# One launch of attention and experts: first two stages joined, four stored blocks a side, second key stack loaded by DMA

## Time and profile before

| | |
|---|---|
| median of 3 runs | 1906.98 us |
| the profiled execution | 1909.95 us |
| its span | 1908.0 us |
| TensorE busy | 87% of the span |
| VectorE, ScalarE, GpSimd busy | 73%, 60%, 56% |
| mean DMA rate | 237 GB/s |
| spread and project end, attend begins | 195.6 us |
| mix begins | 1396.6 us |
| experts begin | 1592.5 us |

### The profile page before, as it was taken

How to read it: one execution, slowest core, us unless ns; L and a number is a source line. 1 busy time by engine, 2 the same in 40 slices (tenths; PEclk the granted TensorE clock), 3 DMA queues, 4 the chain that set the end, 5 groups by cost and what they waited for, 6 DMA issues and landing times. The chain is left out here.

```text
span 1908.0 us, 41019 instructions
## 1 busy us (share of the span) xinstructions
PE 1656.5 (87%) x13688; PEld 1140.5 (60%) x13688; DVE 1390.5 (73%) x3938; ACT 1151.0 (60%) x2745; POOL 1071.8 (56%) x1268
## 2 busy tenths in 40 slices
PE   1883289999999999999999999999944755999997
PEld 1442056666666666666666666666523645999996
DVE  1573099999999999999999999999823652434343
ACT  1673258888888888887887888888622540222221
POOL 0210187787787787787787787787403521333332
PEclk9997589999999999999999999999976765999998
DMA  3599788878788878778888778878259823676772
GB/s 106 183 301 306 221 287 285 282 261 286 259 259 291 281 258 287 262 257 289 286 257 282 267 257 278 270 258 278 64 126 275 268 76 137 210 215 215 224 211 74
DMA packets 320830, 452.57 MB, mean 237 GB/s; under 512 B 38204, under 2 KB 260303, under 8 KB 320526
## 3 DMA queue, kind: packets, MB, share of 16 engines
q1 hardware_dynamic: 308034, 414.42, 67.6%
q10 hardware_dynamic: 7596, 21.10, 3.6%
q0 software_dynamic: 4992, 14.43, 2.1%
HBM read 256.87 MB, written 193.27 MB: 236 GB/s over the span
## 5 line engine op out<-in xcount | busy, mean ns | idle before, releaser
L872 ACT ACTIVATE t_probsT<-t_flip 128x512 f32<-128x512 f32 x1024 | 626.2, 614 | 200.3 <-PE t_flip L766 141.8
L817 DVE TENSOR_REDUCE t_most<-t_scores 128x1 f32<-128x640 f32 (+1 forms) x512 | 435.4, 850 | 58.1 <-PE t_scores L743 54.5
L836 DVE TENSOR_SCALAR t_band<-t_band,t_top 128x384 f32<-128x384 f32 (+1 forms) x512 | 415.5, 812 | 0.0
L780 PE MATMUL t_sum_ps<-t_probsT,t_vals 128*32 128x256 f32 x4096 | 327.2, 391 | 0.2 <-ACT t_probsT L872 0.2
L864 ACT COPY t_table<-t_table_ps 128x388 f32<-128x388 f32 x512 | 247.9, 484 | 65.3 <-issue 40.9
L949 POOL TENSOR_TENSOR t_near<-t_near,t_masks 128x768 f32<-128x768 f32 (+1 forms) x128 | 270.4, 2113 | 0.0
L821 DVE CUSTOM_DVE_ANT_0 t_band<-t_scores,t_near 128x384 f32<-128x384 f32 (+1 forms) x512 | 262.0, 512 | 0.0
L766 PE MATMUL t_flip<-t_masks,t_band 128*128 128x128 f32 x1408 | 260.6, 274 | 0.0
L736 PE MATMUL t_scores<-t_after,t_quest 105*128 105x256 bf16 (+3 forms) x1024 | 243.3, 287 | 3.8 <-DVE t_most L821 3.6
L743 PE MATMUL t_scores<-t_masks,t_near 128*128 128x128 f32 x1408 | 241.1, 274 | 1.6 <-POOLq L952 1.5
L743 PEld LDWEIGHTS t_scores<-t_masks,t_near 128*128 128x128 f32 x1408 | 180.7, 142 | 40.9 <-POOLq L952 2.8
(11 more groups left out here) (187 smaller groups left out, 2569.7 us busy)
## 6 DMA issues: line engine op xcount, KB each, us to landing
skew_d<-t_table SPq DMA_DIRECT2D x128, 1024.0 KB, 7.1
t_near<-skew_d SPq DMA_DIRECT2D x128, 640.0 KB, 8.1
t_near<-skew_d SPq DMA_DIRECT2D x128, 384.0 KB, 6.4
e_w<-in_L_ffn_W_dram ACTq DMA_DIRECT2D x39, 512.0 KB
e_w<-in_L_ffn_W_dram SPq DMA_DIRECT2D x39, 512.0 KB
split_d<-p_part SPq DMA_DIRECT2D x32, 384.0 KB
t_after<-split_d SPq DMA_DIRECT2D x64, 192.0 KB
t_quest<-split_d SPq DMA_DIRECT2D x64, 192.0 KB
```

Of the source, the lines that this page charges most:

```text
L780: last = nc.tensor.matmul(sum_ps[32 * g:32 * g + 32, 0:2 * P], vals[b % 2][:, j, h * VDIM:h * VDIM + 32], probsT[s % 3][:, g * 2 * P:(g + ...
L817: nc.vector.tensor_reduce(most[:, c, 1:2], out[:, wide:S], AX.X, ALU.max)
L836: nc.vector.tensor_scalar(band[n % 2][:, t, 0:wide], band[n % 2][:, t, 0:wide], top[n % 2][:, t:t + 1], None, ALU.subtract).then_inc(level ...
L872: nc.scalar.activation(probsT[s % 3][:, half * 512:(half + 1) * 512], flip_ps[half][:, :], ACT.Exp, scale=SCALE).then_inc(expd, 1)
```

## The change

1. spread goes, and its work is done at the beginning of project, in project's buffers. posT_d goes too, and the columns of far_w are written in SBUF. The masks are loaded once, kept in one buffer for all blocks, and so are the rows of pick_d. ScalarE's copy of the first turned group (L501) moves ahead of the next group's normalisation. The semaphores of project are cleared in attend behind the first loads.
2. xn_d, its loads in mix and GpSimd's addition go. 1 / deviation of each token stays in SBUF (inv_all), and mix adds x * inv_all instead of xn, with two instructions of VectorE for one. (The mean's share is the same for all features of a token, and falls out in the normalisation that follows.) bo is added by a matmul with a row of ones, two a group.
3. split_d has four blocks a side instead of six, so a group is stored with eight transfers instead of twelve, and the far parts with one instead of four.
4. A stack of 96 rows is loaded by two transfers of 48, each with three blocks on the DRAM side, and where a part is wanted three times the step of that dimension is 0. before is loaded in the same way; twin goes. The far rows of two units come together, in three transfers (load_far).

```diff
-QSLOTS = ((0, 1, 3), (3, 1, 2), (5, 1, 1))
-KSLOTS = ((1, 2, 3), (2, 2, 2), (0, 1, 1))
+BLOCKS = 4
+QSLOTS = ((0, 3, 4), (1, 5), (2,))
+KSLOTS = ((0, 1, 2), (3, 5), (4,))
...
-        spread(nc, sem, Wk, bk, rel_emb, c_pick, c_masks, c_side, pick_d, posT_d)
...
 # project, SyncE
-                    for m in range(4):
-                        for n, (first, step, many) in enumerate((QSLOTS, KSLOTS)[m // 2]):
-                            at = ((m // 2 * TERMS + first) * (N * DH) + b * D + m % 2 * P) * S + half * G
-                            sp.dma_start(view(split_d, at, [[S, P], [step * N * DH * S, many], [1, G]]),
-                                         part[g % 2][:, n, m, :].unsqueeze(1).to_broadcast([P, many, G])
-                                         ).then_inc(split_out[g % 2], 16)
+                    for m in range(4):
+                        mine = at + m // 2 * (BLOCKS * part_at) + m % 2 * (P * S)
+                        takes = ((0, 3, 1), (0, 1, 0)) if m < 2 else ((0, 3, 0), (1, 2, 3))
+                        for a, z, slot in takes:
+                            sp.dma_start(view(split_d, mine + slot * part_at, [[S, P], [part_at, z - a], [1, G]]),
+                                         part[g % 2][:, a:z, m, :]).then_inc(split_out[g % 2], 16)
...
 # project, ScalarE
+            def keep_x(g):
+                act.wait_ge(x_turned, g + 1)
+                if g >= 2:
+                    act.wait_ge(v_made, g - 1)
+                nc.scalar.copy(xT[g % 2][:, :, :], xT_ps[:, :, :]).then_inc(xT_made, 1)
...
             for s in range(-2, NG + 1):
+                if s == -1:
+                    keep_x(0)
...
 # attend
-    HATS = 5
+    HATS = 6
+    FARS = 2
+    ROW = DH * PARTS
...
-                for dst, side_at in ((after[i], TERMS * part), (quest[i], 0)):
-                    sp.dma_start(dst[0:KROWS, :], view(split_d, side_at + n * (DH * S), [[part, TERMS], [S, DH], [1, S]])
-                                 ).then_inc(hats_in[i], 16)
-                for dst, far_at, many in ((quest[i][FAR:FAR + 6, :], n * (2 * far), 2 * PARTS),
-                                          (after[i][KROWS:FAR, :], (N + n) * (2 * far) + far, PARTS),
-                                          (before[i][KROWS:FAR, :], (N + n) * (2 * far), PARTS)):
-                    sp.dma_start(dst, view(far_d, far_at, [[S, many], [1, S]])).then_inc(hats_in[i], 16)
+                at_q, at_k = n * (DH * S), BLOCKS * part + n * (DH * S)
+                for dst, at, step in ((after[i][0:ROW, :], at_k, 0), (after[i][ROW:KROWS, :], at_k + part, part),
+                                      (quest[i][0:ROW, :], at_q + part, part), (quest[i][ROW:KROWS, :], at_q, part),
+                                      (before[i][0:ROW, :], at_k, 0), (before[i][ROW:KROWS, :], at_k + part, part)):
+                    sp.dma_start(dst, view(split_d, at, [[step, PARTS], [S, DH], [1, S]])).then_inc(hats_in[i], 16)
+
+            def load_far(n):
+                i = n % BUFS
+                if n >= BUFS:
+                    sp.wait_ge(flipped, 2 * QT * (n + FARS - BUFS))
+                far_q = ((n // H * 4 + n % H // 8) * 32 + n % 8 * 2) * far
+                far_k = far_q + 2 * 32 * far
+                for dst, far_at, many in ((quests[FAR:FAR + 6, i:i + FARS, :], far_q, 2 * PARTS),
+                                          (afters[KROWS:FAR, i:i + FARS, :], far_k + far, PARTS),
+                                          (befores[KROWS:FAR, i:i + FARS, :], far_k, PARTS)):
+                    sp.dma_start(dst, view(far_d, far_at, [[S, many], [2 * far, FARS], [1, S]])
+                                 ).then_inc(far_in[i // FARS], 16)
...
                     load_unit(u + 4)
+                if 0 <= u + 2 < N and u % FARS == 0:
+                    load_far(u + 2)
...
-            def twin(n):
-                i = n % BUFS
-                act.wait_ge(hats_in[i], 16 * HATS * (n // BUFS + 1))
-                nc.scalar.copy(before[i][0:KROWS, :], after[i][0:KROWS, :]).then_inc(twin_made, 1)
...
 # mix, VectorE
-                nc.vector.tensor_tensor(y1[g % BUFS][:, :, :], out_ps[g % 2][:, :, :], xn[g % BUFS][:, :, :],
-                                        ALU.add).then_inc(y1_made, 1)
+                for t in range(G):
+                    tile = g * G + t
+                    last = nc.vector.scalar_tensor_tensor(y1[g % BUFS][:, t, :], xt[g % XBUFS][:, t, :],
+                                                          inv_all[:, tile:tile + 1], out_ps[g % 2][:, t, :], ALU.mult, ALU.add)
+                last.then_inc(y1_made, 1)
...
 # mix, TensorE
+                    last = nc.tensor.matmul(out_ps[g % 2][:, t, :], masks[0:1, 3, :], bo_row[:, :], start=False, stop=True)
...
 # experts, SyncE
-                if s == 0:
-                    sp.dma_start(masks[:, :, :], c_masks).then_inc(loaded, 16)
```

More of the change, by code:

```diff
@@ L115, in build @@
         bias_d, total_d = dram("bias_d", [E, HID]), dram("total_d", [E, D])
-        spread(nc, sem, Wk, bk, rel_emb, c_pick, c_masks, c_side, pick_d, posT_d)
[L118 to L122, removed]
+        masks = ctx.enter_context(nc.sbuf_tensor("masks", [P, 5, P], F32))
+        inv_all = ctx.enter_context(nc.sbuf_tensor("inv_all", [P, NT], F32))
+        with nc.sbuf_tensor("rows", [KROWS, H, 2, FEW], BF16) as rows:
+            project(nc, sem, x, Wq, bq, Wk, bk, Wv, bv, rel_emb, c_pick, c_masks, c_side, pick_d, split_d, far_d, v_d,
+                    masks, inv_all, rows)
+            spent = sem.spend()
+            attend(nc, sem, spent, masks, rows, split_d, far_d, v_d, skew_d, ctx_d)
         sem.take_back(spent)
@@ L273, in project @@
-def project(nc, sem, spent, x, Wq, bq, Wk, bk, Wv, bv, bo, c_masks, posT_d, xn_d, split_d, far_d, v_d):
+def project(nc, sem, x, Wq, bq, Wk, bk, Wv, bv, rel_emb, c_pick, c_masks, c_side, pick_d, split_d, far_d, v_d,
+            masks, inv_all, rows):
     G = 512
@@ L333, in load @@
                              ).then_inc(x_in[g % XB], 16)
[L335 to L340 removed]
+            front = [(rel[:, :], rel_emb), (masks[:, :, :], c_masks), (wk[:, :, :], Wk.rearrange("(k p) n -> p k n", p=P)),
+                     (bk_row[:, :], bk.rearrange("(a n) -> a n", a=1)), (side[:, :, :], c_side),
+                     (pick[:, 0, :], c_pick[0, :, :]), (pick[:, 1, :], c_pick[1, :, :])]
+            assert len(front) == 7
+            loads = [(wq[:, :, :], Wq.rearrange("(k p) n -> p k n", p=P)),
                      (wv[:, :, :], Wv.rearrange("(k p) n -> p k n", p=P)),
@@ L547, in _, with attend @@
                 last.then_inc(far_made, 1)
-        @block.gpsimd
-        def _(pool):
-            pool.wait_ge(loaded, 16 * 9)
-            for g in range(NG):
-                pool.wait_ge(xn_made, GT * (g + 1))
-                if g >= 2:
-                    pool.wait_ge(xn_out[g % 2], 16 * (g // 2))
-                nc.gpsimd.tensor_tensor(xnb[g % 2][:, :, :], xn[g % NB][:, :, :],
-                                        bo_b[:, :].unsqueeze(1).to_broadcast([P, GT, D]), ALU.add).then_inc(xnb_made, 1)
-def attend(nc, sem, spent, c_masks, split_d, far_d, v_d, pick_d, skew_d, ctx_d):
+def attend(nc, sem, spent, masks, rows, split_d, far_d, v_d, skew_d, ctx_d):
     AHEAD = 2 * QT + QT // 2
```

293 lines of the change are left out of this document (121 added, 172 removed).

## The result

The changed kernel takes 2043.9 us in the median of four runs (2041.7 to 2046.0), the kernel before 1906.8: a ratio of 1.0715, 95% interval 1.0697 to 1.0734. It is slower by 137 us; the forecast was 2039. The profiled execution took 2043.8 us, its span is 2042.0, against 1909.95 and 1908.0.

A forecast was written before the change was run, and what follows sets the result against it. TensorE sets the pace, DMA is runner-up; after the change three DMA engines would bind attention. 1909.95 - 59 + 198 + 3 - 8 - 2 = 2042 us profiled, 2039 as median; range of 8 in 10: 1940 to 2190.

The forecast's parts named there:

- The front: Before attend: first product at 20 us instead of 53.2, groups at 12.4 us, attend beginning 59 us earlier.
- Attention: Loads on three DMA engines slow each unit from 17.8 to 21.0 us: +198 us over 62 units, bounds 105 and 347.
- +3 for the start: First skew transfers of attention stand behind a load of 8 us instead of 2.7: +3 us (0 to 6).
- my two ends: Time of one of the three engines per attention unit: 19.5 us from below, 23.4 us from above.
- near 0.2 for some 8 us a unit: Sign in attention that the forecast is right: DMA share stays near 3 of 16 for some 8 us each unit.
- mix: Fewer xn transfers outweigh the added bo matmuls: -8 us, from -14 to +5.
- +2: In mix, the two added bo matmuls a group cost 2 us, counted only in the last four groups.
- experts: Masks no longer stand before the first total in SyncE's queue: -2 us, from -4 to 0.
- (a): Attention loads do not bind, by a wrong three-engine spread or air in the queue: 1838 us, chance 0.09.
- (b): In attention ScalarE holds TensorE back, hidden by busy time, and loads do not bind: 1771 us, chance 0.01.
- (c): In attention waits for near let TensorE's clock fall, units taking 25 us: 2297 us, chance 0.12.
- (d): Three engines bind in attention, but the front gains only its start: 2060 us, chance 0.78 together with the forecast.

The follow-up runs named there:

- 318 kB with 16 engines: The changed kernel with the rows of a stack reordered, so each load has outer dimension 16 instead of 3: 1869.8 us (ratio 0.9796).
- the kernel with 16 and twin: The changed kernel with loads of outer dimension 16, and before copied by ScalarE again instead of loaded: 1860.8 us (ratio 0.9750).
- bo first: The changed kernel with loads of outer dimension 16, ScalarE's copy of before restored, and mix's bo matmuls ahead of the wait for heads: 1839.8 us (ratio 0.9640).
- the attention part alone: The kernel before with six loads of 48 rows a unit, outer dimension 3, no step 0, and twin removed: 2090.3 us (ratio 1.0946).

## Why the prediction was right, point by point

**The front: right.** First product at 19.61 (20), groups of 12.4 us (34.43 to 46.82), last parts stored from 127.23 (127.6), attend's first load at 135.60 (137), and -60.0 for -59. The last stores were a little quicker than 0.81 us an issue: 4.43 us for eight. That ScalarE's chain holds at the start of attend held too: it copies first at 154.41, 5.6 us behind TensorE's first table.

**Attention: right in mechanism, a little large.** +198 and +3 for the start stood against +185.5: 20.8 us a unit for 21.0, and nothing seen of the 3. The engines ran at 23.0 GB/s (478 kB in 20.8 us), between my two ends of 24.5 (478 kB in 19.5) and 20.4. My 21.0 lay between the two ends by choice, and that it came so close is partly luck. I had put the distance from the low end down to idle engines, but with 4 of 1040 rows under 0.19 little of it seems to be that; more likely an engine carries less in the mixed traffic of a unit than in the rows that I had taken, which no run shows apart. The sign "near 0.2 for some 8 us a unit" was too long: 226 of the 1040 rows are at 0.26 or below, 4.5 us a unit, since the skew transfers overlap the loads. What stays open is why 318 kB with 16 engines cost 11 us and 347 kB in the kernel before none: its mean share is 0.89 for 0.82 and GpSimd waits 108 us for near instead of 9, so a second limit, that of the whole queue, may lie close. I left it out when I wrote that to drop twin is worth nothing: to replace it by loads costs 9 us, even with 16 engines.

The Trainium skill, "DMA: Bandwidth & Descriptors", section "Why a DMA increments its semaphore by 16 and not by 1", has the number of engines as the largest up to 16 that divides the slowest dimension of both sides. The trace agrees with it for 6 (0.39), 3 (0.19 to 0.21) and 2 (0.12, 0.13).

**mix: wrong in sign, -8 forecast and +16.2 measured.** The step that failed is "+2" for the bo matmuls. I saw them as free in all but the last four groups, because TensorE waited 3 to 4 us of each group for transfers, and put +5 as upper end with them on the path of all. Sixteen groups of 2.44 us are 39, so that end was far too low for what it named. Measured: mix +16.2, and 26 us less without the matmuls (on the kernel with 16 and twin, whose mix is 1 us longer). Two things took the cover away. VectorE's residual waits for the group's last matmul, and it stands ahead of the next heads, so bo behind the products lengthens a chain through two engines even while TensorE has idle time. And TensorE stayed at 0.50 up to 1655 us, where the kernel before reached 0.91. With bo first the chain gets shorter and the clock higher at once, so no run tells how much is due to each. Rows of the kernel before, PE, PEld, DVE, ACT, POOL busy, clock, share, GB/s:

```profile
1461.00:1495.00 34.00, 20.50 (x72) 16.35 (x72) 16.60 (x73) 16.18 (x36) 14.87 (x12) 0.65 0.92 290
1509.00:1528.00 19.00, 16.39 (x130) 12.46 (x130) 14.02 (x54) 12.92 (x29) 11.17 (x9) 0.91 0.85 281
```

The rest of the term came out about right: with no bo matmul mix takes 102.7 us, 9 less than in the kernel before, for the 10 (7 and 3) that I had put for the transfers that go; no run takes these transfers alone. My 8.8 us a group was that of groups 7 to 10 only: from the product of group 4 (1446.18) to that of 11 (1503.37) it was 8.2. The matmuls ate the gain and 16 us more.

**experts.** The interval from the last product in mix to experts is 6.6 us shorter; 2.9 of it are the shorter wait for total (4.15 for 7.08). The rest I didn't take apart.

**The forecast as a sum.** 2042 for the profiled execution and 2043.8 measured are closer than the steps: attention was 15 us too high and mix with experts 19 too low (-10 forecast, +9.0 measured), and the two errors cancel. The size of the total is no evidence for either.

**The rivals.** (a), loads that don't bind, and (b), ScalarE, fell: the loads bound, and the copy was worth keeping. (c) happened in part: the clock fell in about every second unit (0.50 at 812), and TensorE waited 47 times, 2.0 us in the mean. The fall did not add: units with it take 20.7 us and units without it 20.8, so what it cost TensorE was taken off its wait. The Trainium skill, "TensorE: Matmul & The Clock Gate", section "HAM oscillation — how this bites in real kernels", tells of a clock that falls in the wait for DMA in each tile. The trace agrees for the wait of 2.60 us at 809.95; behind the wait of 2.41 at 851.38 the row from 852 to 853 reads 1.00. (d) fell with 12.4 us a group.

## What to carry to other kernels

Count DMA traffic for each of the 16 engines, not in the mean: give every transfer an outer dimension of 16 or a multiple of it (here 16 in DRAM, with 48 rows in SBUF), and look in the 1 us stretches for a share of k/16 that stands still. Here the order of two dimensions was worth 174 us, more than the whole loss of 137. A matmul added to a group can be paid by the engine that waits for the group's end, so put what needs no input ahead of the wait. An engine's idle time is no room for work before one has followed its ring to the end: GpSimd idled 4 us a group and had none to give.

## What was not expected of the hardware

TensorE ran at half clock for 52 us in which it was busy without a break (1603 to 1655 us, 0.50), and with the same matmuls in another order it had 0.88 in groups 11 to 13, the last three of that stretch. In the changed kernel it came back to full clock during the 64 short matmuls of L1326 (0.86 from 1659 to 1661). A busy engine alone does not bring the clock back here; what does, these runs don't tell.

A repeated source (step 0) cost little, if anything: the attention part alone, without it, cost 177 us (1356.0 less 1178.9), the changed kernel, with it, 185.5. The two also differ in their far loads and in how split_d is stored, so the 8 us between them belong to no one part.
